# Seven products of half size in place of eight: Strassen's algorithm for the projections of a lightning-attention kernel

## The reference, cut to what matters

```python
x = layernorm(hidden_states)                      # 4 batches, 512 tokens, 512 features
qkv = silu(x @ w_qkv.T)                           # 16 heads; q, k, v of 128 each
# per head, blocks of 64 tokens, kv starts at zero:
o = (q * q_decay) @ kv + ((q @ k.T) * diag_decay) @ v
kv = block_decay * kv + (k * k_decay).T @ v
out = norm_w * o * rsqrt(mean(o * o over all heads) + 1e-6)
s = (sigmoid(x @ w_gate.T) * out) @ w_out.T
g = silu(x * sum(top8) + top8_weights @ expert_bias)   # softmax router over 64 experts
result = hidden_states + s * g
```

## Time and profile before

| | |
|---|---|
| median of 3 runs | 1169.78 us (1168.41 to 1170.02) |
| span of the profiled execution, first to last instruction | 1168.3 us |
| granted TensorE clock, mean over the span | 0.996 of full |
| PE busy | 1145.2 us |
| DVE busy | 853.2 us |
| POOL busy | 501.4 us |
| ACT busy | 358.5 us |
| moved by DMA | 56.06 MB |

### The profile page before, as it was taken

The page is one execution under the profiler, slowest core; times in us unless marked ns, Lnnn a source line. Parts: engine busy times, 40 slices in busy tenths (PEclk is TensorE's granted clock), DMA queues, the critical chain, the costliest instruction groups (busy, mean ns, idle before and its releaser), DMA issues.

```text
span 1168.3 us, 17546 instructions
## 1 busy us (share of the span) xinstructions
PE 1145.2 (98%) x6700; PEld 1008.8 (86%) x6700; DVE 853.2 (73%) x1703; ACT 358.5 (31%) x584; POOL 501.4 (43%) x412
## 2 busy tenths in 40 slices
PE   8999999999999999999999999999999999999996
PEld 7888888888888888888878888888888888888885
DVE  7777768767667775766997687776676766677677
ACT  4443333323232322323223333332222232323221
POOL 6353342534435443452664434335253443535343
PEclk9999999999999999999999999999999999999999
DMA  5010110111201111110322201102010110201012
GB/s 183 30 44 31 28 64 19 37 55 36 91 19 54 31 44 37 36 54 20 108 89 77 71 19 38 37 19 73 19 46 28 37 55 19 73 19 36 19 36 90
DMA packets 19250, 56.06 MB, mean 48 GB/s; under 512 B 2528, under 2 KB 2656, under 8 KB 19168
## 3 DMA queue, kind: packets, MB, share of 16 engines
q1 hardware_dynamic: 19168, 54.94, 15.0%
HBM read 50.74 MB, written 4.19 MB: 47 GB/s over the span
## 4 chain that ended last, share of the span: by engine, by line
PE 90%; DVE 8%; issue 1%; DMA 0%; ACT 0%; SPq 0%; POOL 0%; ACTq 0%; DVEq 0%
PE PB L238 18%; PE PB L239 18%; PE PB L240 18%; PE PY L238 5%; PE PY L240 5%; PE PY L239 5%; PE PT L795 2%; PE PO L826 2%; PE PS L726 2%; PE PS L238 1%; PE PO L825 1%; PE PS L240 1%; PE PS L239 1%; PE PO L830 1%; PE PO L829 1%
## 5 line engine op out<-in xcount | busy, mean ns | idle before, releaser
L238 PE MATMUL PB<-XH,WH 128*128 128x512 f32 x768 | 304.4, 396 | 0.0
L239 PE MATMUL PB<-XL,WH 128*128 128x512 f32 x768 | 300.2, 391 | 0.0
L240 PE MATMUL PB<-XH,WL 128*128 128x512 f32 x768 | 299.9, 390 | 0.0
L399 POOL TENSOR_TENSOR WL<-STG,WH 128x1024 fp32r<-128x1024 f32 (+1 forms) x64 | 153.5, 2398 | 138.2 <-DVE WH L388 138.2
L853 POOL TENSOR_TENSOR SS<-SS,GF 128x512 f32<-128x512 f32 x63 | 81.3, 1291 | 289.7 <-ACT GF L849 289.7
L240 PEld LDWEIGHTS PB<-XH,WL 128*128 128x128 f32 x768 | 144.4, 188 | 31.3
L238 PEld LDWEIGHTS PB<-XH,WH 128*128 128x128 f32 x768 | 144.7, 188 | 27.5
L239 PEld LDWEIGHTS PB<-XL,WH 128*128 128x128 f32 x768 | 145.0, 189 | 27.1
L674 POOL TENSOR_TENSOR QL<-Q,QH 128x256 fp32r<-128x256 f32 x128 | 103.9, 832 | 111.1 <-DVE QH L670 111.1
L238 PE MATMUL PB<-WH,XH 128*128 128x256 f32 x512 | 147.0, 287 | 0.9 <-DVE XL L493 0.6
L240 PE MATMUL PB<-WH,XL 128*128 128x256 f32 x512 | 144.8, 283 | 0.0
(11 more groups left out here) (195 smaller groups left out, 2218.1 us busy)
## 6 DMA issues: line engine op xcount, KB each, us to landing
STG<-in_wp SPq DMA_DIRECT2D x80, 512.0 KB, 3.6
XG<-in_x SPq DMA_DIRECT2D x16, 256.0 KB, 4.3
XF<-in_x SPq DMA_DIRECT2D x12, 256.0 KB, 3.3
out<-Y SPq DMA_DIRECT2D x12, 256.0 KB, 2.2
STG<-in_x SPq DMA_DIRECT2D x4, 256.0 KB, 3.3
out<-STG SPq DMA_DIRECT2D x4, 256.0 KB, 2.1
XF<-in_eb SPq DMA_DIRECT2D x2, 128.0 KB, 4.9
XF<-in_rw SPq DMA_DIRECT2D x1, 128.0 KB, 6.0
```

Source lines behind the costliest of these rows:

```text
L238: eng.matmul(o, ah, bh, start=first, stop=False)
L239: eng.matmul(o, ah, bl_, start=False, stop=False)
L240: return eng.matmul(o, al, bh, start=False, stop=last)
L399: do(en, lambda e, a=a, b=b, d=d: e.tensor_tensor(lo[:, a:b], STG[:, n % NSTG, a:b], f32(hi[:, a:b]), ALU.subtract).then_inc(d[0], 1))
```

## The change

The projections of a group (V, Q and K of head 0, the gates, Q and K of head 1) are a matrix product of four quarters: two output blocks of 128 features (`o`) by two batches (`b`), over a contraction of 512 that is cut in two halves. The new kernel does each by Strassen's algorithm in Winograd's form: seven products of half the contraction (two tiles of 128, so 6 matmuls of 512 columns each) in place of eight. For it

- `x_turn` turns the same token tile of both batches, and makes besides X11, X21, X22 (`XH[:, 0:6]`) four sums T1 to T4 (`XH[:, 6:14]`) on DVE. `XH` and `XL` hold one half's X alone; at the change of halves `turns(1, after)` makes it anew, with pieces of attention called in between.
- `w_sums` makes four sums of weight quarters on POOL, `w_parts` the casts on ACT and the differences on POOL, two groups ahead.
- `product` runs one of the seven. Products 1 and 2 add up in the bank `BA` (C11); ACT copies `BA` after product 1 into the group's chain bank `BS`, where 6, 7 and 4 add up, with ACT copies after 6 and 7 (to C12's and C22's places in SBUF); product 5 goes to `BD`, DVE adds `BD` to C22, then product 3 adds to the same `BD`, and DVE adds it to C12. The order on PE is 6, 2, 7, 3, then 1 of the next group, 4, then 5 of the next group; `inserts(s)` stands between them, seven slots per group, 28 per pair of heads.
- V comes out with features on partitions; `v_turn` turns it by four transposes into the bank `PX`, per head and batch.
- The inter term multiplies the split Q with the state, and DVE scales the result in PSUM (`inter`); the intra term adds to it (`intra`). `qd_parts` is gone.
- The decay tables are made eight heads at a time in `Y`'s place, stored to a DRAM tensor `dqd`, and loaded back per pair (`dq_load`).
- Y parts, router, `v_turn`, norm and final tiles share one bank `PX`. The x tiles come anew through a ring of five buffers `XR`; `g` is made per tile just before its use (`g_make`, `final_at`), for half 0 in the slots from `base + 15` on, for half 1 after everything else.
- Casts of Q, K and weights go to ACT, differences of Q and P to DVE.

The new file is mostly rewritten. The lines that the change turns on (`op` appends an instruction to an engine's program and returns the token that `wait` waits for; `dma` appends a transfer to SP's):

```diff
-                    for a in range(4):
-                        s = slice((k % 2) * 512 + a * 128, (k % 2) * 512 + (a + 1) * 128)
-                        i = mm3(e, bank[:, :], WH[:, k // 2, s], WL[:, k // 2, s], xh[:, a, :], xl[:, a, :],
-                                a == 0, a == 3)
...
+PROD = {1: (A11, X11), 2: (A12, X21), 3: (AS4, X22), 4: (A22, XT4), 5: (AS1, XT1), 6: (AS2, XT2), 7: (AS3, XT3)}
...
+            free = None
+            for g in range(2):
+                hs = slice(8 * g, 8 * g + 8)
+                wait("dve", free)
+                a = op("dve", lambda e, hs=hs: e.tensor_tensor(
+                    tmp, ixq.unsqueeze(1).to_broadcast([128, 8, DQW]),
+                    NS[:, hs].unsqueeze(2).to_broadcast([128, 8, DQW]), ALU.mult))
+                wait("act", a)
+                a = op("act", lambda e: e.activation(tmp, tmp, ACT.Exp))
+                wait("pool", a)
+                a = op("pool", lambda e: e.affine_select(
+                    out=tmp[:, :, 0:C], in_=tmp[:, :, 0:C], compare_op=ALU.is_ge, fill=0.0, base=0,
+                    pattern=[[0, 8], [1, C]], channel_multiplier=-1))
+                wait("sp", a)
+                free = dma(s_dqs, lambda e, hs=hs: e.dma_start(dqd[:, hs, :], tmp))
+            tk["dqs"] = free
...
+            wait("act", turned[0], tk.get("x_old"), tk.get(("at", t % 2)), tk.get("vt_old"))
+            ca = op("act", lambda e: e.activation(at_, a, ACT.Copy))
+            ha = op("act", lambda e: e.activation(XH[:, 0:4, s], a, ACT.Copy))
+            wait("dve", turned[1], ca, tk.get("tt"), tk.get("vt_old"))
+            t1 = op("dve", lambda e: e.tensor_tensor(tt[:, 0:2, :], b[:, 0:2, :], at_[:, 0:2, :], ALU.subtract))
+            wait("dve", t1)
+            t2 = op("dve", lambda e: e.tensor_tensor(tt[:, 2:4, :], b[:, 2:4, :], tt[:, 0:2, :], ALU.subtract))
...
+            wait("dve", t2, ha)
+            t4 = op("dve", lambda e: e.tensor_tensor(tt[:, 6:8, :], a[:, 2:4, :], tt[:, 2:4, :], ALU.subtract))
+            t3 = op("dve", lambda e: e.tensor_tensor(tt[:, 4:6, :], tt[:, 2:4, :], at_[:, 0:2, :], ALU.subtract))
+            la = op("dve", lambda e: e.tensor_tensor(XL[:, 0:4, s], a, f32(XH[:, 0:4, s]), ALU.subtract))
+            wait("dve", hb)
+            lb = op("dve", lambda e: e.tensor_tensor(XL[:, 4:6, s], b[:, 2:4, :], f32(XH[:, 4:6, s]), ALU.subtract))
+            wait("act", t3)
+            ht = op("act", lambda e: e.activation(XH[:, 6:14, s], tt, ACT.Copy))
+            wait(low, ht)
+            lt = op(low, lambda e: e.tensor_tensor(XL[:, 6:14, s], tt, f32(XH[:, 6:14, s]), ALU.subtract))
...
+        def w_sums(g):
+            c, k = divmod(g, 4)
+            n = 5 * c + k
+            src = STG[:, n % 2, :]
+            a11, a12, a21, a22 = (src[:, i * 256:(i + 1) * 256] for i in range(4))
+            s1, s2, s3, s4 = (ST[:, i * 256:(i + 1) * 256] for i in range(4))
+            wait("pool", tk["stg", n], tk.get("st_h"), tk.get("st_l"))
+            a = op("pool", lambda e: e.tensor_tensor(s1, a21, a22, ALU.add))
+            op("pool", lambda e: e.tensor_tensor(s3, a11, a21, ALU.subtract))
+            wait("pool", a)
+            a = op("pool", lambda e: e.tensor_tensor(s2, s1, a11, ALU.subtract))
+            tk["s3", g] = a
+            wait("pool", a)
+            tk["s4", g] = op("pool", lambda e: e.tensor_tensor(s4, a12, s2, ALU.subtract))
...
+        W_PARTS = [(0, 2, "stg", 0, 2), (2, 5, "s3", 0, 3), (5, 6, "s4", 3, 4), (6, 7, "stg", 3, 4)]
...
+        def product(g, q):
...
+            wb, xb = PROD[q]
+            chain = BS[g % 2]
+            bank = BA if q in (1, 2) else BD if q in (5, 3) else chain
+            first = q in (1, 5)
+            wait("pe", tk["w", g, wb])
+            for t in range(4):
+                wait("pe", tk["xa" if xb < 3 else "xt", h, t])
+            if q == 1:
+                wait("pe", tk.get("ba_free"))
+            elif q == 5:
+                wait("pe", *tk.get("bd_free", ()))
+            elif q in (6, 2):
+                wait("pe", tk["seed", g])
+            elif q == 7:
+                wait("pe", tk["u2", g])
+            elif q == 3:
+                wait("pe", tk["c22", g])
+            elif q == 4:
+                wait("pe", tk["u3", g])
...
+            def pe(e):
+                for kt in range(2):
+                    w = slice(wb * 256 + kt * 128, wb * 256 + (kt + 1) * 128)
+                    i = mm3(e, bank[:, :], WH[:, u, w], WL[:, u, w], XH[:, 2 * xb + kt, :], XL[:, 2 * xb + kt, :],
+                            first and kt == 0, q in (2, 3, 4) and kt == 1, True)
+                return i
+            tk["prod", g, q] = d = op("pe", pe)
+            if q == 1:
+                wait("act", d, tk.get(("bs_free", g % 2)))
+                tk["seed", g] = op("act", lambda e: e.activation(chain[:, :], BA[:, :], ACT.Copy))
+            elif q == 6:
+                dst = place(g, 0, 1)
+                wait("act", d, *place_free(g, 0, 1))
+                tk["u2", g] = op("act", lambda e: e.activation(dst, chain[:, :], ACT.Copy))
+            elif q == 2:
+                tk["ba_free"] = evict(g, 0, 0, BA, d)
+            elif q == 7:
+                dst = place(g, 1, 1)
+                wait("act", d, *place_free(g, 1, 1))
+                tk["u3", g] = a = op("act", lambda e: e.activation(dst, chain[:, :], ACT.Copy))
+                wait("dve", a, tk["prod", g, 5])
+                tk["c22", g] = op("dve", lambda e: e.tensor_tensor(dst, dst, BD[:, :], ALU.add))
+                evict(g, 1, 1, None, tk["c22", g])
+            elif q == 3:
+                dst = place(g, 0, 1)
+                wait("dve", d, tk["u2", g])
+                a = op("dve", lambda e: e.tensor_tensor(dst, dst, BD[:, :], ALU.add))
+                tk["bd_free"] = (a,)
+                evict(g, 0, 1, None, a)
+            elif q == 4:
+                tk["bs_free", g % 2] = evict(g, 1, 0, chain, d)
...
+        def v_turn(c, r, b):
+            wait("pe", tk["vt", c, r, b], tk["ident"], *tk.get("px", ()))
+            def pe(e):
+                for t in range(4):
+                    s = slice(t * C, (t + 1) * C)
+                    m = e.transpose(PX[:, s], VT[:, r, b, s], ident[:, :])
+                return m
+            d = op("pe", pe)
+            tk["vt_read", r, b] = d
+            src = PX[:, :].rearrange("p (c k n) -> p c k n", c=2, k=2)[:, :, 0, :]
+            wait("act", d, tk.get(("v_read", b)))
+            a = op("act", lambda e: e.activation(V[:, b, :, :], PX[:, :].rearrange("p (t n) -> p t n", t=4), ACT.Copy))
+            a = op("act", lambda e: e.activation(VH[:, b, :, :], src, ACT.Copy))
+            wait("dve", a)
+            a = op("dve", lambda e: e.tensor_tensor(VL[:, b, :, :], src, f32(VH[:, b, :, :]), ALU.subtract))
...
+        def inter(c, r, b):
+            s = slice(2 * C, 4 * C)
+            wait("pe", tk["kv"], *tk.get("po", ()))
+            tk["inter"] = d = op("pe", lambda e: mm3(e, PO[:, s], KVH[:, :], KVL[:, :], QH[:, s], QL[:, s],
+                                                     True, False, True))
+            wait("dve", d, tk["dq", c])
+            tk["scaled"] = op("dve", lambda e: e.tensor_tensor(PO[:, s], PO[:, s], DQ[:, c % 2, r, C:3 * C], ALU.mult))
...
+        def final(h, b, t, tile, dst, g, en="pool"):
+            ap, tok, k = tile
+            wait("dve", g, tk["rr", b], tk["ya", b, t])
+            a = op("dve", lambda e: e.scalar_tensor_tensor(dst, Y[:, b, t, :], rr[:, b, t:t + 1], dst,
+                                                           ALU.mult, ALU.mult))
+            tk["y_read", b, t] = a
+            wait(en, a, tok)
+            a = op(en, lambda e: e.tensor_tensor(ap, ap, dst, ALU.add))
+            wait("sp", a)
+            o = dma(s_out[k], lambda e: e.dma_start(out[2 * h + b, t * 128:(t + 1) * 128, :], ap))
+            xr_free[k] = o
...
+            for r, s in ((0, 7), (1, 21)):
+                for b, o in ((1, (3, 5, 6, 8, 9, 11)), (0, (9, 11, 12, 14, 15, 16))):
+                    for f, k in zip((split_qk, scores, states, inter, intra, gate), o):
+                        plan(base + s + k, f, c, r, b)
+            plan(base + 8, v_turn, c, 0, 1)
+            plan(base + 11, v_turn, c, 0, 0)
+            plan(base + 19, v_turn, c, 1, 1)
+            plan(base + 24, v_turn, c, 1, 0)
+            for b, ss in ((1, (34, 35, 37, 38)), (0, (40, 41, 43, 44))):
+                for t, s in enumerate(ss):
+                    plan(base + s, ypart, c, b, t)
...
+        for i, (b, t) in enumerate([(1, 0), (1, 1), (1, 2), (1, 3), (0, 0), (0, 1), (0, 2), (0, 3)]):
+            plan(base + 15 + 3 * i, g_make, 0, b, t)
+            plan(base + 17 + 3 * i, final_at, 0, b, t)
...
+                    load_tiles(h, t)
+                banks = [(BA, (tk.get("ba_free"),)), (BD, tk.get("bd_free", ()))]
+                la, lb = x_turn(h, t, tile_of[h, t], banks, "pool" if h == 0 else "dve")
```

(23 more changed lines are left out.)

1561 lines of the change are left out of this document (591 added, 970 removed).

## The result

The changed kernel takes 1471.51 us (median of 4, 1468.39 to 1474.44), the one before 1169.1 in the same comparison: ratio 1.259, 95% interval 1.256 to 1.262. The forecast was 1315 (1240 to 1380): the direction was right, the size, +145 us of some +302, was half of the true one. The profiled execution has a span of 1466.7 us against 1168.3, so 298.4 us are to be placed.

The account below looks back on a forecast made before the run. PE's queue of matmuls, 98% busy, was taken as the bound. 1168.3 - 66 + 45 + 37 + 32 + 19 + 20 + 58 = 1313 us, plus 1.5 around the span: 1315, range 1240 to 1380.

Parts of the forecast that it names:

- The start (+45): Before the first product: it waits for all token tiles and decays, running near 60 us against 15; +45 us.
- the end (+58): After the last projection: last head's chain stands alone, then eight serial output tiles of 8.3 us each; +58 us.
- The wait of product 3 (+37): Inside each group: product 3 waits for DVE's addition to C22; 2.3 us per pair, x 16, +37 us.
- PE's work (-66): On PE throughout: fewer product matmuls -96, V transposes +28, router logits +2; net -66 us.
- Other waits of the steady part (+32): Groups 2 and 3: scores wait for the decay chunk and the Q and K split, about 1 us each; +32 us.
- What the other engines get: Engine loads: DVE about 60 us less, ACT about +370, POOL about +45; none becomes the bound by its load.
- rival (d): Throughout: DVE's queue, held by POOL, falls behind; each of 16 pairs waits 4 us more; 1379 us, 11%.
- Rival (c): In the pairs: PE's clock falls in the gaps, 1.7 us lost once per pair, +27; 1342 us, 15%.
- Between the halves (+19): Change of halves: four tile pairs need 20 us of DVE plus 15 of attention work, against 16 of PE; +19 us.
- statistics and finals (+20): Half 1's statistics, half 0's finals: DVE waits for late loads, twelve waits of 3 us, half under PE's lead; +20 us.
- (b): In the groups: the waits are hidden, those at the ends are not; 1246 us, 17%.
- the forecast's own signs: Wrong if first product starts before 45 us, end tiles overlap, or PE's DVE waits leave 2 to 6 us per pair.

Follow-up runs that it names:

- experiment 9: Changed kernel with late split of output weights and x-tile loads one ahead in tail, statistics and half 0's finals: 1363.7 us; also without POOL's weight differences: 1355.0.
- Experiments 2: Changed kernel with the split of the output weights four slots later (slot 22, not 18): 1421.4 us against 1471.5.
- experiment 3: Changed kernel with POOL's weight differences left out from group 2 on: 1413.4 us; with the split of the output weights four slots later as well: 1404.9.
- experiment 4: Changed kernel with eight unused matmuls per pair of heads directly ahead of the intra term that waits: 1464.5 us.
- experiment 5: Changed kernel with x-tile loads issued one tile ahead: in the tail alone 1448.2 us; for half 1's statistics and half 0's final tiles 1432.6.
- experiment 8: Unused matmuls ahead of turns between halves, changed kernel: 1480.1 us. Half 0's last four Y parts moved among half 1's products, three-edit kernel: 1352.1 against 1363.7.

## Why the forecast was half of the truth

**The start (+45) and the end (+58): right in kind, and in size in part by luck.** The first product runs at 59.98 us (60 forecast), with DVE waiting 9.1 us for the store. But its parts were off and made up for each other: two pairs of tiles done at 30.3 us and not 32, 15.9 and not 18 us for the decays, 13.8 and not 10 for the other two pairs. From the last product to the end it is 96.3 us (89 forecast): some 38 us until the first tile's own work and not 24, then tiles 7.3 us apart and not 8.3. By the ledger, start and end together are 105 against 103.

**The wait of product 3 (+37): right in the clean pairs.** 1.50 us in group 3 (1.65 forecast), 0.35 in group 0 (0.4), nothing in group 1 (0.25). Each wait costs about 0.23 more than its row (an estimate from the rows): the matmul ahead ends 0.39 and not 0.23 after its start, and the first one behind it keeps the next 0.31 away. That gives 2.3 us per pair, the forecast's number. Behind the change of halves the same wait is up to 8.4 us, and makes its sum over the kernel 34.2.

**PE's work (-66): too good by some 20.** A clean pair was 68.7 us; less 6.0 of products and with 1.75 of V turns it should be 64.45. In the kernel with three edits (experiment 9) a clean pair of 70.4 has 3.4 us of waits and 5 x 0.23 beside them, which leaves 65.85. The 1.4 us more, x 16, were not traced further. Nor did the forecast see PE's busy time: 1180 us and not 1080, with 269.5 us of the span at 1.2 GHz.

**Other waits of the steady part (+32): the step that failed for the pairs.** The two waits it named are there, and small: 0.4 us for the decayed chunk and 0.8 for the split of K (1 and 1 forecast), and 0.7 for Y's bank. The largest one of a pair is missing from it: the 2.1 us for the scaled inter term. The forecast costed the scaling at nothing, as DVE work under PE's products; it did not name what stands ahead of it in DVE's queue, the split of the output weights at slot 18, nor that its result is needed at slot 22. Experiments 2 and 3 show that this wait is made by the queue's order and by POOL's hold together. The hold itself had been seen in the earlier trace rows and set beside the words "what is queued ahead of them may not": that was the case, and it carried no price. Of the 69 us that the twelve ordinary distances grew, 37 go with the late split. Of the 32 that stay, 20 are in the four pairs beside the router's work, for which 2 were forecast and which no experiment took apart, and 12 in the others, which is about the 1.4 us each from above.

**What the other engines get: wrong, and rival (d) was weighed by it.** POOL was to gain 45 us and gained 148 (501.4 to 649.4): the sums of weights (lines 358 to 364) take 3.4 us per group of heads, in pieces of 256 columns, and not the 2.42 of one operation of 1024. DVE was to lose 60 us and gained 6 (853.2 to 859.1), 49 of it the hold of experiment 3. "60 us less load" was the argument against (d).

**The clock.** Rival (c) was true in kind and priced well: 1.5 us per fall by experiment 4, against 1.7; but it came in five of the eight pairs without router work, and not in each. It came behind the wait that rival (d) is about, so the two were not alternatives. Together they give 1315 + 27 + 64 = 1406 as the forecast priced them. The Trainium skill (TensorE: Matmul & The Clock Gate, A second HAM failure mode) tells of a kernel whose short idle times between groups of matmuls make the clock fall and rise again and again. The trace agrees in these five pairs (0.98 in a pair with the 2.1 us wait, 1.00 in the same pair with the filler) and not in the other three, which have the same wait at 1.00. The Trainium skill (GPSIMD Engine Reference, Key points) says that GpSimd contends with VectorE instructions in a 2-port mode or with two SBUF inputs. The trace agrees for operations on SBUF (576 to 410 ns for the cast once POOL does less), and for the scaling, whose one input is in PSUM, it shows no hold (427 and 428 ns).

**Between the halves (+19), and statistics and finals (+20): the step that failed for the rest.** 39 were forecast and 117 measured, less 3 x 6.1 that these distances share with every pair: 99, so 60 too few. Two causes are shown. The loads issued late cost 39 us and not 20 (experiment 5): the twelve waits of 3 us "half of it under PE's lead" were waits of up to 7.9 us on DVE in the statistics, behind which PE waited 7.5 and 6.4 us, so no lead of PE was left. And PE's order in front of the first product of half 1 cost 11.6 (experiment 8). A change of 45.7 us against 35 is left, by the order of the program the turns' own chain from PE over ACT and DVE, which was not tried. That makes 42 of the 60; the other 18 were not separated. POOL's weight differences have a part in it: 12 us in these distances even with the x loads ahead (experiment 9). What PE's low clock costs there stays open, since the filler of experiment 8 did not bring the clock back at the end of the stretch.

**The rivals' weights.** (b), all waits in the groups hidden, had 17%, more than (c) or (d), and the truth lay 225 us above it. The range ended at (d), as if only one more thing could go wrong. Every wait was priced alone, by its own chain from a free DVE, while the changed kernel feeds PE from queues in which each lateness reaches the next. With three queues put in order the kernel takes 1363.7 us, and with the change's order as well 1352.1, which is inside the range. That does not make the sum right: it held the tail's serial loads in its +58 and 20 us for those in the middle, and two of the edits take these away. The kernel with the late split alone, 1421.4, is the one to set beside the sum, and is 106 above it. Nor did the forecast's own signs speak: it would call itself wrong if PE's waits for DVE passed 6 us per pair, and a clean pair has 5.8 where the sum had priced 4.3 (only the four beside the router's work have 6.8 to 9.3). A sign must stand near the price that it guards.

## What to carry to other kernels

When a result is needed by PE a few slots after it is made, read the queue of the engine that makes it, and price every instruction between the two slots, held ones at their held time; moving one split by four slots was worth 50 us. Do not pull work ahead to cover a wait without asking what that work was covering: twice (product 1, the decays) the wait came back longer behind it. Counted in matmuls, a seven-product scheme saves 6.0 us of 68.7 per pair here, 4.25 after the V turns; in the trace 2.85 of them are left (68.7 less 65.85), and the five waits of such a mended pair, each its row plus about 0.23 us, cost 4.6.
